# Groups 4 to 7 of a matmul pass by Strassen's seven products, and another order of the narrow matmuls

## What is computed

```python
base  = einsum('bsi,oi->bso', x, W)
low   = einsum('bsi,bir->bsr', x, lora_A[label])      # 5 labels, rank 32
x = x + base + 0.5 * einsum('bsr,or->bso', low, lora_B_w)
P = dtA[:, :, None] * arange(512)
K = 2.0 * einsum('hn,hnl->hl', Ct, exp(P)).real
y = irfft(rfft(x, n=1024) * rfft(K, n=1024))[..., :512] + x * D
x = x + y * (arange(512) < length)
```

## Time and profile before

| | us |
|---|---|
| median of 3 runs | 192.66 (192.64 to 192.76) |
| the profiled execution | 192.58 |
| its span, first to last instruction | 190.9 |

### The profile page before, as it was taken

How to read it: one execution, slowest core, us unless ns; L and a number is a source line. 1 busy time by engine, 2 the same in 40 slices (tenths; PEclk the granted TensorE clock), 3 DMA queues, 4 the chain that set the end, 5 groups by cost and what they waited for, 6 DMA issues and landing times.

```text
span 190.9 us, 2653 instructions
## 1 busy us (share of the span) xinstructions
PE 185.6 (97%) x933; PEld 156.6 (82%) x933; DVE 125.9 (66%) x164; ACT 91.3 (48%) x144; POOL 68.7 (36%) x111
## 2 busy tenths in 40 slices
PE   7799999999999999999999999999999999999994
PEld 2487887888888888888888888888999999999993
DVE  0599979458977048858607407279987777786743
ACT  2456066254148754154463312766565656565600
POOL 6038840000000268100000000379886666676600
PEclk9999999999999999999999999999999999999999
DMA  6999990000000000000001600045988788897433
GB/s 191 349 366 422 424 408 11 0 0 2 3 2 0 0 2 3 0 0 0 0 3 34 200 0 0 0 146 167 309 285 295 282 261 291 277 274 270 181 139 138
DMA packets 14797, 27.35 MB, mean 143 GB/s; under 512 B 2592, under 2 KB 5056, under 8 KB 13888
## 3 DMA queue, kind: packets, MB, share of 16 engines
q1 hardware_dynamic: 14064, 25.81, 39.1%
q10 hardware_dynamic: 720, 1.38, 2.1%
HBM read 18.71 MB, written 8.47 MB: 142 GB/s over the span
## 4 chain that ended last, share of the span: by engine, by line
PE 95%; DVE 2%; ACT 1%; issue 0%
PE y_ps L553 13%; PE y_ps L554 12%; PE y_ps L555 12%; PE k_ps L620 10%; PE k_ps L621 10%; PE k_ps L622 10%; PE low_ps L547 4%; PE low_ps L549 4%; PE low_ps L548 4%; PE y_ps L560 4%; PE y_ps L569 2%; PE y_ps L573 2%; PE y_ps L577 2%; PE low_ps L526 2%; PE k_ps L536 1%; PE k_ps L555 1%
## 5 line engine op out<-in xcount | busy, mean ns | idle before, releaser
L406 POOL TENSOR_TENSOR t_lo<-w_raw,t_hi 128x512 fp32r<-128x512 f32 x32 | 44.3, 1393 | 38.0 <-ACT t_hi L468 37.8
L620 PE MATMUL k_ps<-xs_hi,t_hi 128*128 128x128 f32 (+3 forms) x130 | 41.5, 319 | 0.2 <-DVE x_all L829 0.2
L621 PE MATMUL k_ps<-xs_hi,t_lo 128*128 128x128 f32 (+3 forms) x130 | 41.5, 319 | 0.0
L622 PE MATMUL k_ps<-xs_lo,t_hi 128*128 128x128 f32 (+3 forms) x130 | 41.4, 318 | 0.0
L553 PE MATMUL y_ps<-x_hi,w_hi 128*128 128x512 f32 x104 | 40.6, 391 | 0.0
L555 PE MATMUL y_ps<-x_lo,w_hi 128*128 128x512 f32 x104 | 40.6, 391 | 0.0
L554 PE MATMUL y_ps<-x_hi,w_lo 128*128 128x512 f32 x104 | 40.6, 390 | 0.0
L757 DVE COPY_PREDICATED low_sel<-lab_mask,low_ps 32x512 f32<-32x512 int32 x32 | 23.3, 729 | 25.0 <-PE low_ps L549 24.1
L829 DVE COPY_PREDICATED x_all<-len_mask,k_ps 128x512 f32<-128x512 int32 x31 | 23.3, 750 | 13.1 <-PE k_ps L622 13.0
L769 DVE TENSOR_TENSOR xs_lo<-x_all,xs_hi 128x512 fp32r<-128x512 f32 x32 | 28.1, 883 | 4.6 <-ACT xs_hi L462 4.6
L462 ACT CAST xs_hi<-x_all 128x512 fp32r<-128x512 f32 x32 | 19.9, 622 | 19.7 <-PE k_ps L622 19.7
(11 more groups left out here) (132 smaller groups left out, 221.4 us busy)
## 6 DMA issues: line engine op xcount, KB each, us to landing
w_raw<-k_pad SPq DMA_DIRECT2D x32, 256.0 KB, 4.2
out<-x_all SPq DMA_DIRECT2D x31, 256.0 KB, 3.3
x_all<-in_xt SPq DMA_DIRECT2D x7, 1024.0 KB, 12.3
w_raw<-in_wt ACTq DMA_DIRECT2D x4, 256.0 KB, 5.4
x_all<-in_xt SPq DMA_DIRECT2D x4, 256.0 KB, 7.2
ab_raw<-in_ab SPq DMA_DIRECT2D x1, 320.0 KB, 3.7
a_raw<-in_a_lab ACTq DMA_DIRECT2D x1, 320.0 KB, 7.4
out<-x_all SPq DMA_DIRECT2D x2, 128.0 KB, 1.8
```

The source lines that it names most:

```text
L406: g.tensor_tensor(t_lo[:, k % TR, :], t_raw[:, k % RAW, ::-1], f32(t_hi[:, k % TR, :]), ALU.subtract).then_inc(t_lo_done, 1)
L620: mm(o, t_hi[:, u, cols(lag)], xs_hi[:, b, x], start=(lag == 0), stop=False, skip_group_check=True)
L621: mm(o, t_lo[:, u, cols(lag)], xs_hi[:, b, x], start=False, stop=False, skip_group_check=True)
L622: return mm(o, t_hi[:, u, cols(lag)], xs_lo[:, b, x], start=False, stop=ends, skip_group_check=True)
```

## The change

Groups 4 and 5 are one pair, 6 and 7 the other (PAIRS = (4, 6)). X of a pair is cut into quarters of two chunks by four heads: X11 and X21 of the first group, X12 and X22 of the second, W into w11 to w22. By the Strassen-Winograd scheme seven products of quarters (M1 to M7, each 2 output chunks x 2 input chunks x 3 matmuls) take the place of eight. The sums of quarters of W (four, of 512 columns) and of X (T1, T3, T2, T4, in place, of 1024 columns), the low half of X11 and four low halves of weight sums are on GpSimd, the first pair's ahead of its 26 narrow steps. ScalarE casts seven operands of a pair, VectorE subtracts for six, and adds the products (`mix`: one operand in PSUM). `k_scale`, `fac_lo` and the K matmuls move into and behind pair 0, the mask to pair 1, and heads' merges stay in pass 2. The low product of a pair has as many matmuls as before, from the same quarters. In pass 2 each of lag 3's three matmuls (128 columns) stands behind one of lag 0's (512) in place of behind lag 2.

```diff
-MASK_GROUP = 5
-BETWEEN = {}
+PAIRS = (4, 6)
+FIRST = PAIRS[0]
...
+        op_order = ("X11", "X22", "X21", "T3", "T2", "T4", "T1")
+        sum_order = ("T1", "T3", "T2", "T4")
+        m_order = ("M1", "M6", "M5", "M7", "M2", "M3", "M4")
+        mix_order = ("U2", "U3", "C22", "C12", "C21")
+        used_by = {"X11": "M1", "X21": "M2", "X22": "M3", "T4": "M4", "T1": "M5", "T2": "M6", "T3": "M7"}
...
+            pool.wait_ge(w_hi_done, CH + 1)
+            pool.wait_ge(w_lo_done, CH)
+            g.tensor_tensor(w22, w21, w22, ALU.add).then_inc(s_sum, 1)
+            pool.wait_ge(s_sum, 1)
+            g.tensor_tensor(w21, w21, w11, ALU.subtract).then_inc(s_sum, 1)
+            pool.wait_ge(s_sum, 2)
+            g.tensor_tensor(w11, w22, w11, ALU.subtract).then_inc(s_sum, 1)
+            pool.wait_ge(s_sum, 3)
+            g.tensor_tensor(w12, w12, w11, ALU.subtract).then_inc(s_sum, 1)
+            def split_s_lo(n):
+                pool.wait_ge(s_hi_done, n + 1)
+                g.tensor_tensor(s_low[n], s_raw[n], f32(s_high[n]), ALU.subtract).then_inc(s_lo_done, 1)
+            def sums(i):
+                x11, x12, x21, x22 = [raw_of(i, name) for name in ("X11", "X12", "X21", "X22")]
+                pool.wait_ge(op_hi_done, hi_at(i, "X11"))
+                g.tensor_tensor(lo_of(i, "X11"), x11, f32(hi_of(i, "X11")), ALU.subtract).then_inc(x11_lo_done, 1)
+                pool.wait_ge(x_load[PAIRS[i]], 16)
+                pool.wait_ge(x11_lo_done, i + 1)
+                g.tensor_tensor(x11, x12, x11, ALU.subtract).then_inc(x_sum, 1)
+                pool.wait_ge(x_sum, sum_at(i, "T1"))
+                g.tensor_tensor(x12, x12, x22, ALU.subtract).then_inc(x_sum, 1)
+                pool.wait_ge(x_sum, sum_at(i, "T3"))
+                pool.wait_ge(op_lo_done, lo_at(i, "X22"))
+                g.tensor_tensor(x22, x22, x11, ALU.subtract).then_inc(x_sum, 1)
+                pool.wait_ge(x_sum, sum_at(i, "T2"))
+                pool.wait_ge(op_lo_done, lo_at(i, "X21"))
+                g.tensor_tensor(x21, x21, x22, ALU.subtract).then_inc(x_sum, 1)
+            sums(0)
+            pool.wait_ge(k_args, 1)
+            for n in range(3):
+                split_s_lo(n)
...
+            split_s_lo(3)
+            for i in range(1, len(PAIRS)):
+                sums(i)
...
+            def split_op_hi(i, name):
+                if name in sum_order:
+                    act.wait_ge(x_sum, sum_at(i, name))
+                if i > 0:
+                    act.wait_ge(m_done, m_at(i - 1, used_by[follows[name]]))
+                elif name in sum_order:
+                    act.wait_ge(x_used, FIRST - (name in ("T3", "T2")))
+                s.copy(hi_of(i, name), raw_of(i, name)).then_inc(op_hi_done, 1)
...
+                if g == 2:
+                    for n in range(3):
+                        act.wait_ge(s_sum, 4)
+                        s.copy(s_high[n], s_raw[n]).then_inc(s_hi_done, 1)
+                    act.wait_ge(x_load[FIRST - 1], 16)
+                    split_op_hi(0, "X11")
...
+                if g == FIRST - 1:
+                    split_op_hi(0, "T3")
+                    split_op_hi(0, "T2")
...
                 if g != 1:
                     stack_low(g)
+                if g == 2:
+                    act.wait_ge(x_load[FIRST], 16)
+                    act.wait_ge(a_sum_lo_done, 1)
+                    act.wait_ge(b_diff_lo_done, 1)
+                    split_op_hi(0, "X22")
+                    split_op_hi(0, "X21")
...
+            for i, g in enumerate(PAIRS):
+                heads_a = heads_of(g)
+                split_op_hi(i, "T4")
+                split_op_hi(i, "T1")
+                if i == 0:
+                    s.copy(s_high[3], s_raw[3]).then_inc(s_hi_done, 1)
+                if g == PE_KGEN + 1 and i > 0:
+                    copy_k()
+                stack_low(g)
+                act.wait_ge(op_lo_done, lo_at(i, "T4"))
+                for d in range(2):
+                    act.wait_ge(m_done, m_at(i, "M1", d + 1))
+                    s.copy(x_all[:, heads_a, cols(2 + d)], alpha[d].rearrange("p (h b) -> p h b", b=P))\
+                        .then_inc(alpha_read, 1)
+                stack_low(g + 1)
...
+                if i + 1 < len(PAIRS):
+                    act.wait_ge(x_load[g + 1], 16)
+                    act.wait_ge(x_load[g + 2], 16)
+                    for name in ("X11", "X22", "X21"):
+                        split_op_hi(i + 1, name)
+                if g == PE_KGEN - 1:
+                    k_factors_hi()
+                if i + 1 < len(PAIRS):
+                    split_op_hi(i + 1, "T3")
...
+                o, b, u = y2_ps[h % 2], h % XR, h % TR
+                near, far = cols(0), cols(CH - 1)
+                for t, x in ((t_hi, xs_hi), (t_lo, xs_hi), (t_hi, xs_lo)):
+                    mm(o, t[:, u, near], x[:, b, :], start=(t is t_hi and x is xs_hi), stop=False, skip_group_check=True)
+                    mm(o[:, far], t[:, u, far], x[:, b, near], start=False, stop=False, skip_group_check=True)
+                for lag in (1, 2):
+                    last = blocks(o[:, lag * P:L], h, lag, lag, CH - lag, lag == 2)
...
+            def pair(i):
+                g = PAIRS[i]
+                pe.wait_ge(x11_lo_done, i + 1)
+                wait_op(i, "X21")
+                pe.wait_ge(low_read, (NLAB - 1) * (g - 1))
+                low_of(g, True, False, a_hi[:, 0:2, :], a_lo[:, 0:2, :], i, "X11")
+                low_of(g, False, True, a_hi[:, 2:4, :], a_lo[:, 2:4, :], i, "X21").then_inc(low_done, 1)
+                wait_op(i, "X22")
...
+                pe.wait_ge(low_read, (NLAB - 1) * g)
+                low_of(g + 1, True, False, a_sum_hi[:], a_sum_lo[:], i, "X22")
+                wait_op(i, "T3")
+                low_of(g + 1, False, True, a_hi[:, 0:2, :], a_lo[:, 0:2, :], i, "T3").then_inc(low_done, 1)
+                if g == PE_KGEN + 1:
+                    pe.wait_ge(k_copied, 1)
+                elif i == 0:
+                    pe.wait_ge(y_read, CH + 2)
+                if i > 0:
+                    pe.wait_ge(alpha_read, 4 * i)
+                for d in range(2):
+                    product(alpha, d, w11_hi, w11_lo, i, "X11", True).then_inc(m_done, 1)
+                wait_op(i, "T2")
+                pe.wait_ge(s_hi_done, 3)
+                pe.wait_ge(s_lo_done, 3)
+                for d in range(2):
+                    if i > 0:
+                        pe.wait_ge(mixed, mix_at(i - 1, "C21", d + 1))
+                    else:
+                        pe.wait_ge(y_read, CH * (FIRST - 1) + d + 1)
+                    product(beta, d, s_high[1], s_low[1], i, "T2", True).then_inc(m_done, 1)
+                wait_op(i, "T1")
+                for d in range(2):
+                    if i > 0:
+                        pe.wait_ge(mixed, mix_at(i - 1, "C12", d + 1))
+                    else:
+                        pe.wait_ge(y_read, CH * (FIRST - 1) + d + 3)
+                    product(gamma, d, s_high[0], s_low[0], i, "T1", True)
+                    if d == 0:
+                        wait_low(g + 1)
+                    plus_b(gamma, d, b_stack[:, cols(2 + d)], g + 1).then_inc(m_done, 1)
+                for d in range(2):
+                    pe.wait_ge(mixed, mix_at(i, "U2", d + 1))
+                    product(beta, d, s_high[2], s_low[2], i, "T3", False).then_inc(m_done, 1)
+                for d in range(2):
+                    pe.wait_ge(alpha_read, 4 * i + d + 1)
+                    product(alpha, d, w12_hi, w12_lo, i, "X21", False)
+                    plus_b(alpha, d, b_stack[:, cols(d)], g).then_inc(m_done, 1)
...
+                for d in range(2):
+                    pe.wait_ge(mixed, mix_at(i, "C22", d + 1))
+                    product(gamma, d, s_high[3], s_low[3], i, "X22", False)
+                    plus_b(gamma, d, b_diff[:, cols(d)], g + 1).then_inc(m_done, 1)
+                for d in range(2):
+                    pe.wait_ge(mixed, mix_at(i, "U3", d + 1))
+                    product(beta, d, w22_hi, w22_lo, i, "T4", False)
+                    plus_b(beta, d, b_stack[:, cols(2 + d)], g).then_inc(m_done, 1)
...
+            for i in range(len(PAIRS)):
+                pair(i)
+                if PAIRS[i] == PE_KGEN - 1:
+                    pe.wait_ge(alpha_read, 4 * i + 4)
+                    k_matmuls()
...
+            v.tensor_tensor(a_sum, a_diff[:, 0:2, :], a_diff[:, 2:4, :], ALU.add).then_inc(a_summed, 1)
+            dve.wait_ge(b_lo_done, 1)
+            v.tensor_tensor(ab_raw[0:3 * RANK, P:P + HALF], ab_raw[0:3 * RANK, P:P + HALF],
+                            ab_raw[0:3 * RANK, P + HALF:P + L], ALU.subtract).then_inc(b_diffed, 1)
...
                 if g == 2:
+                    dve.wait_ge(a_sum_hi_done, 1)
+                    v.tensor_tensor(a_sum_lo[:], a_sum, f32(a_sum_hi[:]), ALU.subtract).then_inc(a_sum_lo_done, 1)
+                    dve.wait_ge(b_diff_hi_done, 1)
```

(89 more changed lines are left out.)

215 lines of the change are left out of this document (149 added, 66 removed).

## The result

The changed kernel takes 215.77 us in the median (215.20 to 216.43, four runs), the kernel before 192.65 us on the same chip: a ratio of 1.120 [1.117, 1.124]. The profiled execution has a span of 213.8 us, against 190.9.

A forecast was written before the change was run, and what follows sets the result against it. TensorE, 97% busy, was taken as the bound; 5.5 us of matmuls saved were outweighed by waits for VectorE, held by GpSimd. Pass 2 starting at 149.6 us gave a span of 213.7, plus 1.7 around it: 215.4 us, range 198 to 225.

The forecast's parts named there:

- The bound and the path: Whole kernel: TensorE bounds it, 97% busy; group 3's chain through VectorE to the multiplication by B has 1.8 us slack.
- The narrow matmuls at 0: Pass 2: reordered narrow matmuls still take a weight load's length, 0.11 us each, so the new order gains 0.
- Rival (3): Quarter operations cause no holds and pass 2's narrow matmuls' loads hide, -5.0 us: 189.3 us; chance 0.06.
- rival (4): Whole kernel: the change does what its matmul count says and nothing waits, 186.8 us; chance 0.04.
- The hold of 2.2 us for 1024 columns: Beside VectorE's SBUF-SBUF work: each GpSimd quarter operation of 1024 columns takes 2.4 us and holds VectorE for 2.2.
- rival (1): GpSimd's quarter operations: holds don't apply to them, another access pattern, 194.3 us; chance 0.07.
- Rival (2): Shared SBUF path: VectorE keeps it for all it has queued and GpSimd waits, 202.2 us; chance 0.07.
- Step A: Group 2: longer VectorE list and 9.6 us of holds put group 3's select at 68.4 us; TensorE waits 11 us.
- Step B: Filter's chain, groups 4 and 5: late functions and splits bring low parts at 91.5 and 96.6; TensorE waits 3 us.
- Step C: Pair 0's end: k_scale held until 108.5, TensorE waits 6 us for C22, fac_lo ends at 120.6 us.
- Step D: K matmuls 1.4 us, pair 1 26.5 and a wait of 1.1, pass 2 from 149.6 us: span 213.7 us.
- 0 on the sum: Clock after two long waits: half pace may cost 1.6 us each, hidden by VectorE's chain; up to 3 in range.

The follow-up runs named there:

- order_back: The changed kernel with pass 2's narrow matmuls back in the old order (lag 3 behind lag 2): 215.44 us, 1.120 against the kernel before.
- sums_dve: The changed kernel with the low half of X11 and four X sums of each pair on VectorE, not GpSimd: 208.85 us, 1.084 against the kernel before.

## Why the prediction was right, and where its steps were off

**The bound and the path.** The chain that was followed, low product, select, cast, subtract, multiply by B, is the one that broke first. The changed kernel's longest wait stands in front of group 3's multiplication by B, 11.1 us where 11 was written.

**The narrow matmuls at 0.** Right: 1.0002 [0.998, 1.002] alone, heads of 1.90 us. Had all three loads of a head been hidden (-5.0 us), the ratio would have been 0.974. The prediction called the narrow slot a load's length; the rows give a load 0.19 us and 0.11 between starts, and it is the 0.11 that counts. Rival (3) falls with this, rival (4) by the 24.0 us of waits.

**The hold of 2.2 us for 1024 columns.** Right, and it is what carries the forecast. It was extrapolated from instructions of 512 and 64 columns to a length that the trace of before doesn't have. It turned out at 2.2 (3.46 and 3.31 us for steps of 1.25), and rival (1) falls. Rival (2), that VectorE keeps the port, falls by 6.65 us for two subtractions of 1.2.

**Step A.** Select of group 3 at 68.69 (68.4 predicted), multiplication by B at 73.27 (73.0).

**Step B.** Functions of ScalarE at 79.9 (79.6), the reciprocal's end 81.97 (81.5), splits' end 86.8 (87.0), low part of group 4 at 91.3 (91.5), all within 0.5. Group 5's came at 95.93 (96.6): the weight split that I let hold it ran during the select, which reads PSUM. The wait at M5 was 0.9 us in place of 3. Two terms make that up: the low part was 0.7 earlier, and TensorE itself 1.7 later than the 93.4 of the sum (95.1), as it had started 0.3 later and run slower than was put down:

```profile
68.00:73.00 5.00, 0.00 (x0) 0.00 (x0) 3.90 (x6) 1.23 (x2) 3.76 (x3) 0.50 0.00 0
76.00:79.60 3.60, 3.60 (x10) 2.83 (x9) 0.00 (x0) 3.57 (x3) 0.00 (x0) 0.51 0.00 0
79.60:83.00 3.40, 3.40 (x16) 2.79 (x16) 1.38 (x3) 1.03 (x3) 2.39 (x7) 1.00 0.00 0
```

These are windows of the kernel after: during the wait, behind it, and when the clock is back. The clock was taken to be half for 3.2 us, by the warm-up of the earlier trace rows; it was half for 6.3 us, from 73.3 to 79.6, and cost 3.0 us (9.4 us, from 73.27 to 82.63, for 28 matmuls that take 6.4 at full pace), not 1.6. It cost the end nothing, as the sum had said: TensorE waited that much less for group 5's low part.

**Step C.** k_scale ended at 108.2 (108.5), C22 came at 110.1 with a wait of 6.0 (6), and fac_lo at 120.07 (120.6). Behind the C22 wait eight matmuls took 3.5 us instead of 1.8, so 1.7 us in all, hidden behind fac_lo as the sum had put it.

**Step D, the mis-sized terms.** The K matmuls were put at 1.4 us. They had waited 1.9 us for fac_lo and ran at half clock:

```profile
120.30:122.00 1.70, 1.67 (x8) 1.70 (x9) 1.70 (x4) 0.18 (x1) 0.00 (x0) 0.55 0.00 0
```

From the first of the twelve to pair 1's first matmul it was 2.6 us (120.33 to 122.91), 1.2 more than put down (15.9 less 14.6 is 1.3, not 1.4), and pair 1's first three matmuls took 0.4 us more than at full pace: 1.6 us. The step that failed is "0 on the sum" for the clock: it counted two long waits, each with slack behind it, and overlooked the third, short one.

In the other direction, pair 1 had no wait where 1.1 had been put. These two terms belong together, as `order_back` shows, whose code is the same up to pass 2. There the K matmuls ran at full pace (120.79 to 122.28), and TensorE then waited for group 7's low part after all:

```profile
135.52 0.47 PE L905 MATMUL y_ps<-low_stack,b_stack 96*128 96x512 f32 x1 [0.70 <-DVE low_stack L1084]
```

Its pass 2 began at 149.92 us, that of the changed kernel at 150.08. In the changed kernel this low part was there at 135.40 and TensorE came for it at 135.75, late by its slow matmuls; VectorE's select of group 6 had itself waited 0.4 us for it. Without them the multiplication would have started near 135.1, an estimate from these rows, so that 0.6 of the 1.6 us reached the end. The small terms are fac_lo 0.5 early, of which 0.3 arrived at the K matmuls, pass 2 63.7 us (64.1), and 0.2 that pair 1 took beyond its count. That 213.8 agrees with 213.7 to 0.1 is in part luck: terms of 0.2 to 0.6 us happened to cancel, and the four executions alone spread over 1.2 us.

**What stays open.** Why some executions have a half-pace stretch near 8 us, and what sets the length of such a stretch. Why TensorE was 0.9 us late at its 56th matmul in `sums_dve`. That a hold grows with GpSimd's length rests on three lengths, from three different kernels. No run tried the changed kernel with the holds removed and the clock kept up.

## What to carry to other kernels

In these runs an operation that was handed to GpSimd to relieve VectorE was free only where VectorE read PSUM or idled; beside VectorE's SBUF-SBUF work it cost VectorE nearly its whole length (2.2 us of hold against 1.2 us for VectorE doing it itself). Before moving work, list the operations of VectorE in the same stretch and the slack of what it owes next, here 1.8 us. And price every wait of TensorE by its length and the slow matmuls behind it, unless slack follows.
